# Two float32r parts for both tiles of every third pair in the edge stage, with a later addition of the sums

## The reference

```python
h = jnp.maximum(_layernorm(x, axis=-1), 0.0)
msg_input = jnp.concatenate([h[src], h[dst], edge_features], axis=-1)   # 256 + 256 + 16
hid = jax.nn.relu(msg_input @ mW1 + mb1)                                # 50000 x 512
messages = hid @ mW2 + mb2
aggregated = jax.ops.segment_sum(messages, src, num_segments=3125)      # i_idx = src
```

## Time and profile before

| what | value |
|---|---|
| median of three runs | 2148.41 us (2143.78 to 2148.63) |
| the profiled execution's own time | 2150.04 us |
| its span, first to last instruction | 2148.2 us |
| mean granted TensorE clock | 0.914 of 2.4 GHz |
| busy share of PE, DVE, ACT, POOL | 86%, 72%, 37%, 58% |
| edge stage, from the first to the last row of its matmuls | 569 us to 1248 us after the start |

### The profile page before, as it was taken

The page is one execution under the profiler, slowest core; times in us unless marked ns, Lnnn a source line. Parts: engine busy times, 40 slices in busy tenths (PEclk is TensorE's granted clock), DMA queues, the critical chain, the costliest instruction groups (busy, mean ns, idle before and its releaser), DMA issues. The chain is left out here.

```text
span 2148.2 us, 34105 instructions
## 1 busy us (share of the span) xinstructions
PE 1856.5 (86%) x8860; PEld 1252.2 (58%) x8860; DVE 1543.6 (72%) x4318; ACT 795.9 (37%) x1973; POOL 1241.1 (58%) x1461
## 2 busy tenths in 40 slices
PE   3677877775399999999999969998969999999997
PEld 2344454443155555555555536666647788788776
DVE  8877777776299988999988968988877345335332
ACT  0221222221155555555555536655662122113000
POOL 3777777777687777777777739998967000000000
PEclk7676777787699999999999979999999999999999
DMA  5111111111376666666666862212244234343232
GB/s 157 43 55 51 56 56 56 56 56 51 92 199 190 190 191 185 189 190 191 189 188 189 176 187 69 67 63 65 70 119 148 80 114 121 96 120 118 89 118 89
DMA packets 181702, 254.09 MB, mean 118 GB/s; under 512 B 29245, under 2 KB 144762, under 8 KB 181515
## 3 DMA queue, kind: packets, MB, share of 16 engines
q0 software_dynamic: 47888, 126.25, 21.6%
q1 hardware_dynamic: 101186, 99.11, 15.0%
q10 hardware_dynamic: 32440, 26.55, 3.8%
HBM read 202.35 MB, written 49.37 MB: 117 GB/s over the span
## 5 line engine op out<-in xcount | busy, mean ns | idle before, releaser
L971 POOL DMA_INDIRECT brow<-B_rows,rows x440 | 464.8, 1056 | 178.5 <-DVE pre L1074 109.8
L372 POOL DMA_INDIRECT src_list<-ring,ring_row x392 | 400.0, 1021 | 151.5 <-issue 117.6
L1865 PE MATMUL pO<-F,y 128*128 128x512 f32 x1728 | 436.4, 406 | 9.8 <-DVE y L1685 6.6
L1865 PEld LDWEIGHTS pO<-F,y 128*128 128x128 f32 x1728 | 326.8, 190 | 89.0 <-DVE y L1685 6.8
L1002 PE MATMUL pEdge<-A,turned 128*128 x880 | 333.2, 490 | 0.0
L1074 DVE TENSOR_TENSOR pre<-pEdge,brow 128x1024 f32<-128x1024 f32 x220 | 268.7, 1221 | 50.9 <-PE pEdge L1002 42.6
L1230 POOL TENSOR_SCALAR src_oh<-iota,src_s 128x128 bf16<-128x128 bf16 x426 | 281.1, 676 | 31.2 <-PE pC L1401 30.0
L1011 PE MATMUL pNode<-hid_whole,oh 128*128 128x512 f32 x440 | 227.7, 599 | 20.9 <-DVE sums L1092 20.9
L1681 DVE CAST F<-raw 128x512 fp32r<-128x512 uint16 x432 | 173.8, 439 | 66.8 <-PE pO L1865 61.6
L1036 ACT ACTIVATE turned<-pTurn 128x256 fp32r<-128x256 bf16 x220 | 84.8, 386 | 313.3 <-PE pTurn L990 313.3
L1275 DVE TENSOR_SCALAR dst_oh<-iota_cw,dst_s 128x458 bf16<-128x458 f16 x568 | 187.0, 376 | 0.0
(11 more groups left out here) (290 smaller groups left out, 3038.9 us busy)
## 6 DMA issues: line engine op xcount, KB each, us to landing
raw<-C_rows SPq DMA_DIRECT2D x72, 768.0 KB, 4.4
C_rows<-c_rows ACTq DMA_DIRECT2D x175, 114.5 KB, 1.7
rows<-src_list SPq DMA_DIRECT2D x110, 100.0 KB, 2.6
brow<-B_rows,rows POOLq DMA_INDIRECT x440, 3.7
U_parts<-part_u SPq DMA_DIRECT2D x25, 256.0 KB, 2.1
B_rows<-bst SPq DMA_DIRECT2D x25, 256.0 KB, 2.1
src_list<-ring,ring_row POOLq DMA_INDIRECT x392
sums<-U_parts SPq DMA_DIRECT2D x17, 256.0 KB, 5.8
```

Of the source, the lines that this page charges most:

```text
L372: nc.gpsimd.indirect_dma_start(dr.src_list[:, :, :].rearrange("p t w -> (p t) w"), bass.IndirectOffsetOnAxis(ap=ring_row[:, k % RING, t:t ...
L971: nc.gpsimd.indirect_dma_start(brow[:, t % BR, :], None, dr.B, bass.IndirectOffsetOnAxis(ap=rows_i[:, m % LCS, j, 1:2], axis=0)).then_inc( ...
L1865: last = mm(pO[m % 2][half][:, :], y[:, win, part, half * P:(half + 1) * P], F[:, n % FS, :], start=(win == 0 and part == 0), stop=False)
```

## The change

For every third pair (p = 2, 5, 8, ..., 218; 73 pairs; `both(p)`), the first tile too is summed as two float32r parts in place of one float32 product:

- ACT still makes `hid_whole` of it, and `first_upper` in float32r besides. The order on ACT is now upper, whole, first_upper.
- POOL subtracts `first_upper` from `hid_whole` (`first_lower`), behind the gathers.
- PE does the second tile's two products in `node(p)` and the first tile's two in `first_tile(p)`, one iteration later and ahead of the next `node`.
- On DVE `add_pair(i - 5)` stands where `add_pair(i - 4)` stood. The wait of `node` and the number of buffers stay.
- POOL's copies of the index columns go. Every fifth load of rows on SP is followed by a transfer of two columns of 20 tiles from the list straight to `keep.cols` (2560 pieces of 8 bytes; 22 such transfers).
- In `graph_layers`, four semaphores are merged into others.

```diff
-        cols_copied = g.sem("cols_copied")
+        cols_in = g.sem("cols_in")
...
+        def second_used(eng, p):
+            if both(p):
+                eng.wait_ge(second_done, p // EVERY + 1)
+            else:
+                eng.wait_ge(node_done, p + 1)
...
-                    sp.wait_ge(cols_copied, m - LCS + 1)
+                if (m + 1) % CQ == 0:
+                    t = (m + 1 - CQ) * LC
+                    sp.dma_start(keep.cols[:, t:t + CQ * LC, :], dr.src_list[:, t:t + CQ * LC, 0:2],
+                                 allow_slow_non_contiguous=True).then_inc(cols_in, 16)
...
+            def first_lower_part(p):
+                k = p // EVERY
+                pool.wait_ge(first_upper_ready, k + 1)
+                pool.wait_ge(whole_ready, p + 1)
+                if k >= FIRST:
+                    pool.wait_ge(node_done, p - FIRST * EVERY + 1)
+                nc.gpsimd.tensor_tensor(first_lower[:, k % FIRST, :], whole[:, p % WHOLE, :],
+                                        first_upper[:, k % FIRST, :].bitcast(F32), ALU.subtract
+                                        ).then_inc(first_lower_ready, 1)
...
-                    nc.gpsimd.tensor_copy(keep.cols[:, t:t + LC, :], rows[:, m % LCS, :, 0:2]).then_inc(cols_copied, 1)
...
-                pe.wait_ge(whole_ready, p + 1)
-                mm(pN[p % 2][:, :], oh[:, q % OHQ, j, :].bitcast(F32), whole[:, p % WHOLE, :], start=True, stop=False)
+                if not both(p):
+                    pe.wait_ge(whole_ready, p + 1)
+                    mm(pN[p % 2][:, :], oh[:, q % OHQ, j, :].bitcast(F32), whole[:, p % WHOLE, :], start=True, stop=False)
...
+            def first_tile(p):
+                q, j = divmod(2 * p, LC)
+                k = p // EVERY
+                pe.wait_ge(first_upper_ready, k + 1)
+                mm(pN[p % 2][:, :], oh[:, q % OHQ, j, :], first_upper[:, k % FIRST, :], start=False, stop=False)
+                pe.wait_ge(first_lower_ready, k + 1)
+                mm(pN[p % 2][:, :], oh[:, q % OHQ, j, :], first_lower[:, k % FIRST, :], start=False, stop=True
                    ).then_inc(node_done, 1)
...
-            for i in range(PAIRS + 3):
+            for i in range(PAIRS + 4):
                 if i < PAIRS:
                     turn(i)
                 if 0 <= i - 1 < PAIRS:
                     edge(i - 1)
+                if 0 <= i - 4 < PAIRS and both(i - 4):
+                    first_tile(i - 4)
                 if 0 <= i - 3 < PAIRS:
                     node(i - 3)
...
-            for i in range(PAIRS + 5):
+            for i in range(PAIRS + 6):
...
-                if 0 <= i - 4 < PAIRS:
-                    add_pair(i - 4)
+                if 0 <= i - 5 < PAIRS:
+                    add_pair(i - 5)
```

More of the change, by code:

```diff
@@ L54 @@
 LC = 4
-assert NT % LC == 0
+assert NT % (5 * LC) == 0
 CHUNK = 512
@@ L915, in edge_mlp @@
         QUADS = NT // LC
+        CQ = 5
         OHQ = 4
         WHOLE, SPLIT = 3, 2
+        EVERY, FIRST = 3, 1
         rows = g.sb("rows", [P, LCS, LC, ROW])
@@ L932, in edge_mlp @@
         lower = g.sb("hid_lower", [P, SPLIT, HID], F32R)
+        first_upper = g.sb("first_upper", [P, FIRST, HID], F32R)
+        first_lower = g.sb("first_lower", [P, FIRST, HID], F32R)
         pT = [g.ps(f"pTurn{n}", [P, 2 * HID], BF16) for n in range(2)]
@@ L947, in edge_mlp, with both @@
         lower_ready = g.sem("lower_ready")
+        first_upper_ready = g.sem("first_upper_ready")
+        first_lower_ready = g.sem("first_lower_ready")
+        second_done = g.sem("second_done")
         node_done = g.sem("node_done")
         sums_ready = g.sem("sums_ready")
+        def both(p):
+            return p % EVERY == EVERY - 1
+        def second_used(eng, p):
[3 more added lines that the diff above has]
+                eng.wait_ge(node_done, p + 1)
         block = stack.enter_context(nc.Block())
@@ L973, in _ @@
                     bass.IndirectOffsetOnAxis(ap=rows_i[:, m % LCS, j, 1:2], axis=0)).then_inc(b_in[t % BR], 16)
-            pool.wait_ge(cols_copied, QUADS)
+                p = (t - BR) // 2
+                if t % 2 == 1 and p >= 0 and both(p):
+                    first_lower_part(p)
+            for p in range(PAIRS - BR // 2, PAIRS):
+                if both(p):
+                    first_lower_part(p)
         @block.tensor
@@ L1009, in node @@
                     pe.wait_ge(sums_ready, p)
-                pe.wait_ge(whole_ready, p + 1)
-                mm(pN[p % 2][:, :], oh[:, q % OHQ, j, :].bitcast(F32), whole[:, p % WHOLE, :], start=True, stop=False)
+                if not both(p):
+                    pe.wait_ge(whole_ready, p + 1)
+                    mm(pN[p % 2][:, :], oh[:, q % OHQ, j, :].bitcast(F32), whole[:, p % WHOLE, :], start=True, stop=False)
                 pe.wait_ge(upper_ready, p + 1)
-                mm(pN[p % 2][:, :], oh[:, q % OHQ, j + 1, :], upper[:, p % SPLIT, :], start=False, stop=False)
+                mm(pN[p % 2][:, :], oh[:, q % OHQ, j + 1, :], upper[:, p % SPLIT, :], start=both(p), stop=False)
                 pe.wait_ge(lower_ready, p + 1)
-                mm(pN[p % 2][:, :], oh[:, q % OHQ, j + 1, :], lower[:, p % SPLIT, :], start=False, stop=True
+                mm(pN[p % 2][:, :], oh[:, q % OHQ, j + 1, :], lower[:, p % SPLIT, :], start=False,
+                   stop=not both(p)).then_inc(second_done if both(p) else node_done, 1)
+            def first_tile(p):
[5 more added lines that the diff above has]
+                mm(pN[p % 2][:, :], oh[:, q % OHQ, j, :], first_lower[:, k % FIRST, :], start=False, stop=True
                    ).then_inc(node_done, 1)
             pe.wait_ge(sums_ready, 1)
-            for i in range(PAIRS + 3):
+            for i in range(PAIRS + 4):
                 if i < PAIRS:
@@ L1041, in _ @@
                     act.wait_ge(pre_ready, p + 1)
+                    if p >= SPLIT:
+                        second_used(act, p - SPLIT)
+                    nc.scalar.activation(upper[:, p % SPLIT, :], pre[:, p % 2, HID:2 * HID], ACT.Relu
+                                         ).then_inc(upper_ready, 1)
                     if p >= WHOLE:
@@ L1045, in _ @@
                                          ).then_inc(whole_ready, 1)
[L1046 to L1049, removed]
+                    if both(p):
+                        k = p // EVERY
+                        if k >= FIRST:
+                            act.wait_ge(node_done, p - FIRST * EVERY + 1)
+                        nc.scalar.activation(first_upper[:, k % FIRST, :], pre[:, p % 2, 0:HID], ACT.Relu
+                                             ).then_inc(first_upper_ready, 1)
         @block.vector
@@ L1071, in add_target @@
                     dve.wait_ge(upper_ready, p - 1)
+                    if both(p - 2):
+                        dve.wait_ge(first_upper_ready, (p - 2) // EVERY + 1)
                     dve.wait_ge(lower_ready, p - 1)
@@ L1607, in _ @@
                         if n == RAWS - 1:
-                            sp.dma_start(raw_tail[:, :, :], rows[:, 0:LASTW, CHUNKS * CHUNK:N]).then_inc(tail_in, 16)
+                            sp.dma_start(raw_tail[:, :, :], rows[:, 0:LASTW, CHUNKS * CHUNK:N]).then_inc(w_in, 16)
                             for m2 in range(L):
@@ L1841, in heavy_ids @@
                     last = mm(pL[:, 0:2], pick[:, win, :], row_id[:, win, :], start=(win == 0), stop=(win == NW - 1))
-                last.then_inc(id_done, 1)
+                last.then_inc(picks_done, 1)
             def picked(k):
@@ L1851, in picked @@
                               start=(win == 0), stop=(win == NW - 1))
-                last.then_inc(yr_done, 1)
+                last.then_inc(picks_done, 1)
             def tile(k, c, win):
```

15 lines of the change are left out of this document (7 added, 8 removed).

## The result

The changed kernel takes 3061.31 us (median of six runs, 3049.87 to 3080.89) against 2147.85 us for the kernel before (six runs): the ratio is 1.4266, with a 95% interval of 1.4212 to 1.432. The profiled execution took 3056.9 us, its span is 3055.1 us. The forecast was 2915 us in a range from 2690 to 3160.

What follows compares the result with a forecast made beforehand. PE was taken to set the edge stage's pace, with DVE close behind. Turn-taking with the clock at 0.75 adds 765 us and the drain 1 to 2150.0, giving 2916, less 1.6 for the median: 2915 us, range 2690 to 3160.

Steps and rivals of the forecast that it cites:

- The moved addition: Edge stage: DVE's sums behind the target's addition make PE and DVE take turns, 5.79 us in a usual iteration, mean 5.50.
- The stage at the upper clock: Edge stage, first to last target's addition, clock at its upper level: 11 + 215 x 5.50 + 24 = 1218 us, +549.
- The clock: Edge stage: PE's pauses lower the granted clock to 0.75, giving 6.5 us an iteration and a stage of 1433 us, +765.
- The price of the lower level itself: PE's work in a usual edge-stage iteration: the lower clock level adds up to 2.8 us.
- The Trainium skill's advice as a rival: Edge stage: pauses are short, so the clock stays at its upper level; +550 us, about 2700 us; chance 0.17.
- The rival with the lower clock throughout: Edge stage: the clock stays at its lower level, +1088 us, 3236 us; chance 0.09.
- POOL's subtraction: Split pairs on POOL: takes 1.5 to 1.9 us in three pairs, hidden in POOL's idle time.
- The split's 29 us: PE in split pairs: two float32r products for one float32 product save 0.40 us in 73 pairs, if PE sets the pace.
- The rival on the other side: Edge stage: the moved addition does not hold PE up and the split's saving comes through; 2119 us; chance 0.04.
- The column transfers: Row loads on SP: 8-byte pieces take 6 to 9 us a transfer, hidden; uncovered 132 to 198 us; chance alone 0.03.
- Start and drain: Ends of the edge stage: the first four intervals take some 11 us as now, the drain adds about 1 us.

Runs made afterwards that it cites:

- experiment 2: The kernel before with only add_pair(i - 5) in place of add_pair(i - 4) and one DVE iteration more; 3164.34 us, ratio 1.4756.
- experiment 1: The changed kernel with add_pair(i - 4) back at the end of DVE's iteration, the rest of the change kept; 2165.05 us, ratio 1.0091.
- Experiment 4: The changed kernel with add_pair(i - 5) moved to the start of DVE's iteration, the same instruction order as experiment 1; 2167.64 us, ratio 1.0099.
- experiment 7: The changed kernel with the filler products of Experiment 3 and without POOL's subtraction (first_upper taken twice); 2816.1 us, ratio 1.2346.
- experiment 9: The changed kernel with only POOL's subtraction left out (first_upper taken twice); 3051.69 us, ratio 1.4227.
- Experiment 3: The changed kernel with nine (seven where first_tile is) unread filler products on PE between edge and node; 2794.32 us, ratio 1.303.
- version 1: The kernel of experiment 1: the changed kernel with add_pair(i - 4) back; 2165.05 us, ratio 1.0091.
- Experiment 5: version 1 without POOL's subtraction, PE taking first_upper twice; 2288.86 us, ratio 1.0034 against the kernel before on the same chip.
- experiment 6: version 1 with POOL's copies of the index columns in place of the column transfers; 2309.87 us, ratio 1.0109 against the kernel before on the same chip.
- experiment 8: version 1 with every fourth pair split and DVE in place of POOL making first_lower; 2284.39 us, ratio 1.0011 against the kernel before on the same chip.
- experiment 12: The version of experiment 8 with the halved one-hot instructions of experiment 11; 2148.97 us, ratio 1.0019.
- experiment 11: The kernel before with the four-tile one-hot instruction cut in two of two tiles, one in every iteration; 2145.19 us, ratio 0.9997.
- experiment 10: The kernel before with only the 22 column transfers of 8-byte pieces in place of POOL's copies; 2146.64 us, ratio 1.0007.

## Why the prediction was right, and by how much it was off

- **The moved addition.** Right, in place and size. The chain on DVE is 2.54 us as forecast, and PE's part is 3.26 us where the clock is up (forecast 3.25). PE's waits for the sums are 557 us (forecast 500 or more). Alone the moved line makes a ratio of 1.4756 (experiment 2), and taken back it leaves 1.0091 (experiment 1). Experiment 4 adds nothing to this but a repetition.
- **The stage at the upper clock.** Right: forecast 1218 us, measured 1220.3 with the clock held up and the subtraction away (experiment 7). The parts are the forecast's too: 5.78 in a usual iteration and 4.92 in a split one, 0.86 less (forecast 5.79 and 0.86). That the sum comes out to 2 us is luck: the first four intervals took 17.5 us (forecast 11), and the register loads some 20 (forecast 24).
- **The clock.** This is the term that was mis-sized. Of the 146 us between 2915 and 3061, 140 lie in the stage (1573 us, forecast 1433), and the subtraction makes some 7 of them (experiment 9's stage takes 1566). The level was right, 0.74 against 0.75, and this is in part luck: it was taken from the sorting stage, and nothing ahead of the run said that its bursts and pauses should be like these. What failed is the step from the level to the time: "Half of the time at each gives 1 / (0.5 / 5.50 + 0.5 / 8.0) = 6.5 us". That takes the level to be independent of what PE does, and puts 0.5 x 6.5 / 8.0 = 41% of the work at the lower level. In the trace the pauses lie mostly at the upper level and the work mostly at the lower. From the measured spacing, (7.18 - 5.57) / 2.5 = 64% of the work was slow. Counted over the trace, 750 of PE's 1020 busy us in the stage lie at the lower level, which is 58% of the work if PE does half as much in them. The price of the lower level itself was right, 2.74 us in a usual iteration (forecast up to 2.8). Experiment 3 isolates the term: clock 0.97, 267 us less.
- **The Trainium skill's advice as a rival** (TensorE: Matmul & The Clock Gate, "Why this matters for your kernels"), that only longer pauses than these bring the clock down. The trace disagrees: 0.74. The range from 2690 to 3160 us was wide enough to hold this rival's 2700 as well, so it is the trace and experiment 3 that decide against it, and not the range. The rival with the lower clock throughout, 3236 us, lies on the other side of the measured time.
- **POOL's subtraction.** Its duration was 1.27 us (forecast 1.5 to 1.9), and PE never waited for it. "Hidden" was wrong all the same: DVE stands while it runs. The lower part's group grew from 150.0 to 179.3 us. In the changed kernel this is worth little (experiment 9); with the clock up it is most of the 91 us between 1311.0 and 1220.3 (experiments 3 and 7; the lower part's group is 71 us of them), and in version 1 about 21 us (experiments 5 and 6). The Trainium skill names this (GPSIMD Engine Reference, "1. Specifications"): GpSimd shares SBUF interfaces with VectorE and contends with its instructions that have two SBUF inputs. The traces agree, with 2.11 us for 0.68, and with 1.22 us unchanged for the addition that reads PSUM.
- **The split's 29 us.** Not found in any version. The rival on the other side had it in full, since PE sets the pace, and no price for DVE, which is close behind. With the moved addition undone, the ratio is 1.0091 with POOL's subtraction (experiment 1), and 1.0011 and 1.0019 with every fourth pair split and DVE making the lower part (experiments 8 and 12). Experiment 5 has every third pair split and no subtraction, but its extra waits leave open anything between no gain and 14 us. One reading is that PE has 2.94 us of work an iteration and DVE 3.0 or 2.4 by turns, and that the larger of the two counts each time. It is argued and not shown: when experiment 11 took the turns away, nothing was gained. Another is the sum, 0.60 us more on DVE for 0.40 less on PE in a split pair. It fits experiment 12, where DVE is busy 635 of 672 us (575 to 1247 us) and in the kernel before 597 of 667 (575 to 1242 us), but no run isolates it. The third relu's share wasn't tried.
- **The column transfers.** Hidden, as forecast (experiments 6 and 10). The price of a packet, 0.009 us, is a quarter of the estimate's 0.037.
- **Start and drain.** 904 of the 907 us lie between the first and the last target's addition; the rest is 3 us, forecast 1.

## What to carry to other kernels

When a step is moved within one engine's loop, write down for each of its waiters which iteration of the other engine it now depends on: with two buffers, a consumer placed behind an instruction that waits for the producer's same iteration closes a loop, and two engines that overlapped take turns. When pauses come in, price the clock by the work that falls at the lower level and not by the mean level over time. Before an elementwise instruction goes to GpSimd because GpSimd is idle, look at what VectorE does beside it. And an experiment that moves a line across the end of a loop's body may leave the order of instructions as it was: write both orders out before taking the run for evidence.

## What the runs showed of the hardware

- In turns of a pause of 2.5 us and 2.4 to 6.0 us of work, the granted clock was 0.92 in the mean of the pauses and 0.64 in that of the work. The same work took 3.26 us at 1.00 and 6.00 us at 0.50. Filling the pauses with products that nobody reads brought the stage to 0.97 and made the kernel 267 us faster.
- A DVE instruction with two SBUF inputs that meets GpSimd's subtraction ends 0.55 to 0.56 us after the subtraction, in all but a few cases: the lower part then takes 1.67 us and the one-hot instruction 2.11 us, where 0.68 is usual. The subtraction keeps its 1.26 to 1.32 us even where DVE's record begins 0.26 us earlier.
- A transfer of 2560 pieces of 8 bytes lands in 5.0 us, beside gathers that take 62% of the time of the DMA engines, and delays them by 0.2 us.
